# A fused decoder layer on one core: pair 1's softmax sums ahead of a split, a norm ahead of clearing, pair 2's output steps spread among the maxima

## The chip, the core and the metric

The kernel runs on one NeuronCore of one Trainium2 chip. Its engines are TensorE (PE, with its weight loads PEld), VectorE (DVE), ScalarE (ACT), GpSimd (POOL) and SyncE (SP, which here only issues DMAs). Each has an instruction stream of its own that runs in order; they meet at semaphores. The metric is device time in microseconds of one launch.

## The reference, cut to what matters

Inputs are 32 sequences of 64 tokens with 256 channels, and a context of the same shape. The layer is three sublayers, each followed by a residual sum and a layer norm:

```python
x = layernorm(x + self_attention(x))           # 16 heads of 16, causal
x = layernorm(x + cross_attention(x, ctx))     # 64 rows are channels, 256 columns positions: 8 heads of 8, rotary
x = layernorm(x + ffn(x))                      # bitlinear 256->1024, silu, gelu, norm, bitlinear 1024->256
```

The self attention of one pair of sequences is softmax(q k / 4) v, then the output matrix. The cross attention takes q from the normed result, k and v from the context, each projected and biased; q and k are rotated by position before their scores.

## The kernel before, in words

The work is cut into 16 pairs of sequences (`Pair`, `NPAIR`), 128 rows each. Phase A does both attentions, phase B the feed-forward part (from about 350 us on; the change doesn't touch it).

Phase A is a software pipeline. Each engine has a function `prologue()` and then `bodies(eng, body)`, which calls `body(i)` for i = -1, 0, ..., 15; the code is fully unrolled. Turn i has 16 steps s. In it pair i's exponentials are done (`exp_head` L683, `exp_tile` L886), the row maxima of the following tiles run 14 steps ahead (`AHEAD`; `max_head` L655, VectorE's `max_tile` L1080), pair i+2 gets its rotated queries, and pair a = i+3 its self attention. Turn -1 is special: from step 2 on it does the first 14 maxima of pair 0, the rotated queries of pair 1, the value projections for pair 0's cross attention (`xv_proj` L640), and the rest of pair 2's self attention. Pairs 0, 1 and the first half of 2 are done in `prologue()`.

The self attention of a pair goes through these steps, in this order of need:

- `qk_proj` (PE L560) into a bank, `qk_copy` (ACT L840), `k_mask` (L997, POOL, one of pair 0's on DVE), `scores` (PE L578 and L584) into g_b[0] and g_b[1]; before them the previous pair's first statistics instruction must have read g_b[1];
- `row_max` (DVE L1033), `minus_max` (DVE L1041) into `SP`, `self_exp` (ACT L858), `self_sum` (DVE L1050 and reciprocal L1052), `self_norm` (L1007, one instruction 128x1024; DVE for pair 0, POOL for the others);
- `transpose_p` (PE L597), `pt_copy` (ACT L865), `self_pv` (PE L610; it needs the value copies `v_copy`, ACT L848 and L851, and their crossing by DMA, `cross_values` L462), `ao_copy` (ACT L872), `out_proj` (PE L619);
- `norm1_stats` (DVE L1059, L1061, L1063), `rstd` (POOL L328 to L332), `norm1` (ACT L897).

For the cross attention `rotary_proj` (PE L632, L633) multiplies, `rotate` (DVE L1071) applies the tables, and `split_parts` (L1015 to L1025, five instructions, DVE for pair 0's queries, POOL otherwise) makes three bf16 parts. SyncE's `store_parts` (L437) writes them to HBM and `expand_rows` (L452) spreads them over the rows of `QA` and `KA`. Some rows of `KA` must hold ones before that: `ones_rows` (L1002, two memsets a call), for ring slots 0 and 2 on POOL and slot 1 on DVE. After the first eight maxima of a pair `max_transpose` (PE L669), `mt_copy` (ACT L880) and `mt_low` (DVE L1086) make rows that `max_rows` (L481) sends into `QA`; the exponentials of turn 0 need them.

The order on each engine is written out by hand, and an instruction waits for whatever stands before it on its engine. `idle_products(n)` (L791) issues n products of constants, 128x512 bf16, into the bank `u_b`, which nobody reads; they wait for nothing. VectorE's prologue before the change, around the moved lines:

```python
self_norm(dve, nc.vector, p0)
nc.vector.tensor_copy(identh[:], ident).then_inc(s_tab, 1)
ones_rows(nc.vector, 1)
norm1_stats(p0)
```

Of the kernel before, what the change touches and what calls it, by code (L numbers as in the profile page):

```python
# [80 lines left out]
def build_layer(nc, x, xT, ctx, wpT, woT, xW, xB, rows, w1T, w2T, attn_tables, rotary_tables, out):  # L81
    with ExitStack() as outer:
# [462 lines left out]
        def _(pe):  # L545
# [182 lines left out]

            pe.wait_ge(ld_wp, 16)

            def body(i):
                prev, nxt, j, a = i.plus(-1), i.plus(1), i.plus(2), i.plus(3)
                for s in range(16):
# [35 lines left out]
                    if s == 12 and real(a):  # L769
                        transpose_p(a)  # L770
                    if s == 13 and real(a):
                        self_pv(a)
                    if s == 13 and i.v == W_TOTAL:
                        weight_total(2)
                    if s == 15 and real(a):
                        out_proj(a)
                    for n, (turn, step) in enumerate(T_STEPS):
                        if i.v == turn and s == step:
                            pe.wait_ge(s_tab, 4)
                            numbers_transpose(pe, n, use(g_b[2], Event(s_tsb, 0), Pair(0, 0), n + 1)[:, :].bitcast(F16))  # L780
# [5 lines left out]

            def idle_products(n):


                for _ in range(n):  # L790
                    nc.tensor.matmul(u_b[:, :], identb[:], maskb[:].rearrange("p h s -> p (h s)"), start=True, stop=True)  # L791

            def prologue():
                p0, p1, p2 = (Pair(0, n) for n in range(3))
                qk_proj(p0, g_b[2])
                pe.wait_ge(ld_wv, 16)
                v_proj(p0, mx_b[0])
                rotary_proj("k", e_b[0], p0)
                pe.wait_ge(s_tab, 3)
                scores(p0)  # L800
                qk_proj(p1, g_b[2])
                pe.wait_ge(s_init, NINIT)
                idle_products(12)
                transpose_p(p0)
                idle_products(2)
                self_pv(p0)
                idle_products(2)
                out_proj(p0)
                idle_products(2)
                scores(p1)  # L810
                v_proj(p1, mx_b[0])
                idle_products(4)
                rotary_proj("q", mx_b[1], p0)
                rotary_proj("k", e_b[1], p1)
                qk_proj(p2, g_b[2])
                idle_products(12)
                transpose_p(p1)
                idle_products(2)
                self_pv(p1)
                idle_products(2)  # L820
                out_proj(p1)
                idle_products(2)
                scores(p2)
                v_proj(p2, e_b[0])
                rotary_proj("k", e_b[1], p2)
# [7 lines left out]
        def _(act):  # L833
# [93 lines left out]
            def prologue():  # L927
# [8 lines left out]
                norm1(p0)  # L936
                self_exp(p1, 1)
                self_exp(p1, 0)
                v_copy(p1, mx_b[0])
# [7 lines left out]
            def body(i):  # L947
                prev, nxt, j, a = i.plus(-1), i.plus(1), i.plus(2), i.plus(3)
                for s in range(16):
# [14 lines left out]
                    if s == 7 and fresh(a):  # L964
                        self_exp(a, 1)
                        self_exp(a, 0)
                    if s == 9 and real(nxt):
                        mt_copy(nxt, 0, 0)
                    if s == 12 and real(a):
# [3 lines left out]
                    if s == 13 and real(a):  # L973
# [55 lines left out]
        def _(dve):  # L1029
# [94 lines left out]
            def body(i):  # L1124
                prev, nxt, j, a = i.plus(-1), i.plus(1), i.plus(2), i.plus(3)
                for s in range(16):
# [15 lines left out]
                    if s == 9 and real(a):  # L1142
# [11 lines left out]
                    if s == 15 and real(a):  # L1154
# [14 lines left out]
            def prologue():  # L1169
# [10 lines left out]
                ones_rows(nc.vector, 1)  # L1180
# [5 lines left out]
                rotate("q", mx_b[1], p0)  # L1186
                split_parts(dve, nc.vector, "q", p0)
                self_sum(p1)
                rotate("k", e_b[1], p1)
                norm1_stats(p1)  # L1190
# [10 lines left out]
        def _(pool):  # L1201
# [15 lines left out]
            def prologue():  # L1217
# [5 lines left out]
                wait(pool, km[1], p1, 1)  # L1223
                ones_rows(nc.gpsimd, 2)
                pool.wait_ge(s_pad[2], 2)
                rstd(pool, ln1, p0, mv1, rs1)
                self_norm(pool, nc.gpsimd, p1)
# [4 lines left out]
            def body(i):  # L1232
# [6 lines left out]
                if i.v in (NPAIR - 3, NPAIR - 1):  # L1239
                    mean_power(pool, i.v // (NPAIR - 1))  # L1240
                if real(j):
                    split_parts(pool, nc.gpsimd, "q", j)
                if real(a):
# [420 lines left out]
```

## Time and profile before

| | |
|---|---|
| median of 3 runs | 528.34 us (527.87 to 529.71) |
| the profiled execution's own time | 528.22 us |
| its span | 525.7 us |
| TensorE busy | 427.8 us (81%) |
| VectorE busy | 439.2 us (84%) |
| ScalarE busy | 370.2 us (70%) |
| GpSimd busy | 294.2 us (56%) |

The span runs from the first to the last instruction; what lies around it, 2.5 us, is in the time but not in the trace. Busy times don't add up, as the engines work beside each other, and a share is a mean over stages: prologue and turn -1 (to about 62 us), the main loop (to about 350 us), the feed-forward part. A row of a timeline gives the start, the length, and in brackets how long the engine had been idle and what ended that. "PEclk" is the granted clock of TensorE as a share of full speed: 1.00 is 2.4 GHz, 0.50 is 1.2 GHz. Rows merge neighbouring instructions of the same kind, so "x4 2.47" is four in 2.47 us.

### The profile page before, as it was taken

The page shows a single profiled execution, that of the slowest core. Times are in us where ns is not written, and L with a number is a line of the kernel's source. Part 1 is how long each engine was busy: PE and PEld are TensorE (multiplying, and loading weights), DVE is VectorE, ACT ScalarE, POOL GpSimd, SP SyncE. Part 2 cuts the span into 40 slices and gives each one's busy share as a digit, 9 for nine tenths or more (in the row PEclk, how much of TensorE's full clock was granted, in tenths as well). Part 3 has the DMA queues.
Part 4 walks back from the last instruction along what each step waited for, and adds up shares of the span by engine and source line. Part 5 has one row for each costly group of instructions (what it writes and reads, how often), then busy time and mean ns, then how long its engine had stood idle before and what let it go on. Part 6 is the DMA issues. An engine that isn't in the chain of part 4 may idle for free. (4 is left out here: it accounts for less than half of the span.)

```text
span 525.7 us, 11922 instructions
## 1 busy us (share of the span) xinstructions
PE 427.8 (81%) x4130; PEld 231.0 (44%) x4138; DVE 439.2 (84%) x942; ACT 370.2 (70%) x690; POOL 294.2 (56%) x407
## 2 busy tenths in 40 slices
PE   6777899999999999999999999998996602555554
PEld 5453545555555555554545545443432101333332
DVE  2857697988979889799998998988877769999993
ACT  2232366778678786777877767677769878999983
POOL 6744566446474464745557455577232157667653
PEclk9998799999999999999999999999999855555557
DMA  6122313243252422424234232221000000000001
GB/s 222 50 78 65 108 42 112 67 137 113 68 153 66 138 75 65 148 56 139 76 95 144 57 109 63 68 83 52 3 2 0 1 0 1 21 21 20 32 31 40
DMA packets 52459, 37.05 MB, mean 70 GB/s; under 512 B 21552, under 2 KB 47792, under 8 KB 52400
## 3 DMA queue, kind: packets, MB, share of 16 engines
q1 hardware_dynamic: 52112, 36.06, 23.8%
q8 instruction: 33, 0.54, 0.4%
q10 hardware_dynamic: 288, 0.23, 0.2%
q14 instruction: 26, 0.21, 0.1%
HBM read 24.48 MB, written 10.49 MB: 67 GB/s over the span
## 5 line engine op out<-in xcount | busy, mean ns | idle before, releaser
L886 ACT ACTIVATE PB<-e_b 128x512 f32<-128x512 f32 x256 | 148.2, 592 | 59.1 <-PE e_b L683 58.0
L1080 DVE TENSOR_REDUCE MX<-mx_b 128x2 f32<-128x512 f32 x256 | 166.7, 678 | 25.3 <-PE mx_b L655 24.0
L655 PE MATMUL mx_b<-KA,QA 48*128 48x256 bf16 x512 | 98.1, 277 | 11.1 <-DVE MX L1080 10.7
L683 PE MATMUL e_b<-QA,KA 50*128 50x256 bf16 x512 | 97.3, 274 | 0.7 <-ACT PB L886 0.5
L700 PE MATMUL u_b<-PB,VA 128*32 128x256 f32 x1024 | 84.0, 391 | 2.0 <-ACT PB L886 1.7
L1007 POOL TENSOR_TENSOR SP<-SP,srec 128x1024 f32<-128x1024 f32 x15 | 28.5, 1901 | 77.7 <-DVE srec L1052 77.7
L655 PEld LDWEIGHTS mx_b<-KA,QA 48*128 48x128 bf16 x512 | 29.9, 94 | 86.0 <-issue 46.8
L1420 PE MATMUL r_b<-identh,Q 128*128 128x128 f16 x128 | 16.2, 306 | 39.4 <-ACT Q L1333 39.4
L1426 PE MATMUL z_b<-w2q,Q2T 128*128 128x256 bf16 x128 | 28.5, 400 | 19.3 <-ACT Q2T L1344 19.3
L997 POOL TENSOR_TENSOR KM<-QK,att_tab 128x512 f32<-128x512 f32 x31 | 32.0, 1053 | 21.2 <-ACT QK L840 21.2
L560 PE MATMUL g_b<-XT,wp 128*128 128x128 f32 x256 | 34.5, 291 | 4.5 <-DMA wp<-in_wpT 4.5
L1371 POOL TENSOR_TENSOR HHI<-HHI,row_tab 128x1024 f32<-128x1024 f32 x11 | 26.1, 2370 | 19.0 <-ACT HHI L1323 17.9
L700 PEld LDWEIGHTS u_b<-PB,VA 128*32 128x32 f32 x1024 | 22.5, 108 | 30.9 <-ACT PB L886 16.7
L560 PEld LDWEIGHTS g_b<-XT,wp 128*128 128x128 f32 x256 | 31.5, 200 | 7.7 <-DMA wp<-in_wpT 4.5
L1420 PEld LDWEIGHTS r_b<-identh,Q 128*128 128x128 f16 x128 | 12.2, 139 | 46.5 <-ACT Q L1333 46.4
L683 PEld LDWEIGHTS e_b<-QA,KA 50*128 50x128 bf16 x512 | 28.7, 94 | 7.7 <-ACT PB L886 3.6
L328 POOL TENSOR_TENSOR rs<-mv,epsc 128x1 f32<-128x1 f32 x32 | 6.1, 189 | 45.3 <-DVE mv L315 31.6
L865 ACT ACTIVATE PT<-g_b 128x512 f32<-128x512 f32 x32 | 17.5, 595 | 18.2 <-PE g_b L597 17.7
L1426 PEld LDWEIGHTS z_b<-w2q,Q2T 128*128 128x128 bf16 x128 | 15.9, 135 | 28.8 <-ACT Q2T L1344 23.4
L1033 DVE TENSOR_REDUCE smax<-g_b 128x8 f32<-128x512 f32 x32 | 20.6, 686 | 7.4 <-PE g_b L584 7.4
L1041 DVE TENSOR_TENSOR SP<-g_b,smax 128x512 f32<-128x512 f32 x32 | 21.5, 679 | 0.0
L1388 POOL TENSOR_TENSOR root<-base,halves 128x3 f32<-128x3 f32 x17 | 14.5, 856 | 12.4 <-DVE base L1549 12.2
(190 smaller groups left out, 1027.2 us busy)
## 6 DMA issues: line engine op xcount, KB each, us to landing
KA<-parts_k SPq DMA_DIRECT2D x64, 96.0 KB
QA<-parts_q SPq DMA_DIRECT2D x64, 96.0 KB
parts_q<-part_q SPq DMA_DIRECT2D x32, 128.0 KB, 1.9
parts_k<-part_k SPq DMA_DIRECT2D x16, 192.0 KB, 2.1
C<-in_ctx SPq DMA_DIRECT2D x16, 128.0 KB, 3.4
X<-in_x SPq DMA_DIRECT2D x16, 128.0 KB, 2.9
out_y<-O SPq DMA_DIRECT2D x16, 128.0 KB, 1.7
XT<-in_xT SPq DMA_DIRECT2D x15, 128.0 KB, 2.2
```

The costliest lines, as they stand in the source:

```text
L560: last = nc.tensor.matmul(ps[:, P * c:P * c + P], wp[:, k, P * c:P * c + P], XT[:, a.p, k, :], start=k == 0, stop=k == 1)
L655: m = nc.tensor.matmul(mx_b[n % 2][:, D * k:D * k + D], QA[low:low + K_MAX, 2 * i.ring + b, h, P * u:P * u + P], KA[low:low + K_MAX, 2 * i ...
L683: m = nc.tensor.matmul(e_b[n % 2][:, D * k:D * k + D], KA[low:low + K_EXP, 2 * i.ring + b, h, P * sc:P * sc + P], QA[low:low + K_EXP, 2 * ...
L700: last = nc.tensor.matmul(u_b[32 * j:32 * j + 32, D * b:D * b + D], VA[:, i.p, sc, b].rearrange("p h c -> p (h c)")[:, own:own + 32], PB[: ...
L886: nc.scalar.activation(PB[:, n % 4].rearrange("p e t -> p (e t)"), e_b[n % 2][:, :], ACT.Exp, scale=XC ** -0.5).then_inc(e_sb.sem, 1)
L997: ops.tensor_tensor(KM[:, c], QK[:, 2 + c, :].unsqueeze(1).broadcast_to([P, 4, P]), kmask.unsqueeze(2).broadcast_to([P, 4, P]), ALU.mult). ...
L1007: ops.tensor_tensor(SP[:], SP[:], srec[:].unsqueeze(2).broadcast_to([P, SH, SEQ]), ALU.mult).then_inc(s_norm.sem, 1)
L1041: nc.vector.tensor_tensor(SP[:].rearrange("p (c r k) s -> p c r k s", c=2, r=2)[:, :, r], g_b[r][:, :].rearrange("p (c k s) -> p c k s", c ...
L1080: nc.vector.tensor_reduce(MX[:, b, e, 2 * q:2 * q + 2, u], mx_b[n % 2][:, :].rearrange("p (e s) -> p e s", e=2), AXL.X, ALU.max).then_inc( ...
L1371: nc.gpsimd.tensor_tensor(row_h(i), row_h(i), gam, ALU.mult).then_inc(zg.sem, 1)
L1420: m = nc.tensor.transpose(r_b[j.p][:, P * k:P * k + P], low_half(Q2[:, j.p, P * k:P * k + P]), identh[:])
L1426: m = nc.tensor.matmul(z_b[j.p][:, 0:D], Q2T[:, j.p, k, :], w2q[:, k, :], start=k == 0, stop=k == 7)
```

## The change

On TensorE: in turn -1 `transpose_p`, `self_pv` and `out_proj` of pair 2 go from steps 12, 13 and 15 to 8, 9 and 11, and steps 2 to 11 of that turn each end with two idle products; in the prologue four idle products behind `v_proj(p1)` go, and twelve ahead of `transpose_p(p1)` become five. On ScalarE: `v_copy(p1)` goes ahead of `self_exp(p1)`, and pair 2's `pt_copy` and `ao_copy` go to step 8. On VectorE: `ones_rows` of slot 1 goes from ahead of pair 0's statistics to behind pair 1's key rotation; pair 1's sum and its normalisation, which was GpSimd's, come ahead of the queries' split; in turn -1 pair 2's sum goes from step 9 to step 4 and its statistics from step 15 to step 13. On GpSimd: pair 0's `rstd` goes ahead of `ones_rows` of slot 2, pair 1's `self_norm` is gone, and in turn -1 pair 2's `self_norm` goes ahead of the queries' split of pair 1. The number of instructions of the computation stays; idle products go from 40 to 49.

```diff
                         pe.wait_ge(f_sb, f_done(v - 1) - 1 + c)
                     m = first_half(pe, v, c, mx_b[c][:, :])
                 m.then_inc(f_ps.sem, 1)
+
+            def idle_products(n):
+
+
+                for _ in range(n):
+                    nc.tensor.matmul(u_b[:, :], identb[:], maskb[:].rearrange("p h s -> p (h s)"), start=True, stop=True)
 
             pe.wait_ge(ld_wp, 16)
 
...
                         max_transpose(nxt, 0, 0)
                     if s == 12 and real(i.plus(4)):
                         v_proj(i.plus(4), g_b[0])
-                    if s == 12 and real(a):
+                    if s == (12 if i.v >= 0 else 8) and real(a):
                         transpose_p(a)
-                    if s == 13 and real(a):
+                    if s == (13 if i.v >= 0 else 9) and real(a):
                         self_pv(a)
                     if s == 13 and i.v == W_TOTAL:
                         weight_total(2)
-                    if s == 15 and real(a):
+                    if s == (15 if i.v >= 0 else 11) and real(a):
                         out_proj(a)
+                    if i.v < 0 and 2 <= s < 12:
+                        idle_products(2)
                     for n, (turn, step) in enumerate(T_STEPS):
                         if i.v == turn and s == step:
                             pe.wait_ge(s_tab, 4)
...
                     for m in range(7):
                         if real(i) and pv_step(i.v, m) == 16 * i.v + s:
                             pv_quad(i, m)
-
-            def idle_products(n):
-
-
-                for _ in range(n):
-                    nc.tensor.matmul(u_b[:, :], identb[:], maskb[:].rearrange("p h s -> p (h s)"), start=True, stop=True)
 
             def prologue():
                 p0, p1, p2 = (Pair(0, n) for n in range(3))
...
                 idle_products(2)
                 scores(p1)
                 v_proj(p1, mx_b[0])
-                idle_products(4)
                 rotary_proj("q", mx_b[1], p0)
                 rotary_proj("k", e_b[1], p1)
                 qk_proj(p2, g_b[2])
-                idle_products(12)
+                idle_products(5)
                 transpose_p(p1)
                 idle_products(2)
                 self_pv(p1)
...
                 pt_copy(p0)
                 ao_copy(p0)
                 norm1(p0)
+                v_copy(p1, mx_b[0])
                 self_exp(p1, 1)
                 self_exp(p1, 0)
-                v_copy(p1, mx_b[0])
                 qk_copy(p2, g_b[2])
                 pt_copy(p1)
                 ao_copy(p1)
...
                     if s == 7 and fresh(a):
                         self_exp(a, 1)
                         self_exp(a, 0)
+                    if i.v < 0 and s == 8:
+                        pt_copy(a)
+                        ao_copy(a)
                     if s == 9 and real(nxt):
                         mt_copy(nxt, 0, 0)
-                    if s == 12 and real(a):
+                    if s == 12 and real(a) and i.v >= 0:
                         pt_copy(a)
                     if s == 13 and real(prev):
                         norm2(act, prev)
-                    if s == 13 and real(a):
+                    if s == 13 and real(a) and i.v >= 0:
                         ao_copy(a)
                     if s == 15 and real(i.plus(4)):
                         v_copy(i.plus(4), g_b[0])
...
                         minus_max(a, 1)
                     if s == 7 and fresh(a):
                         minus_max(a, 0)
-                    if s == 9 and real(a):
+                    if s == (9 if i.v >= 0 else 4) and real(a):
                         self_sum(a)
                     if s == 9 and real(a) and not fresh(a):
                         rotate("k", e_b[1], a)
...
                         norm2_stats(dve, prev, 1)
                     if s == 14 and real(prev):
                         norm2_max(dve, prev)
-                    if s == 15 and real(a):
+                    if s == (15 if i.v >= 0 else 13) and real(a):
                         norm1_stats(a)
                     if s == 14 and i.v == W_TOTAL:
                         weight_scale()
...
                 self_sum(p0)
                 self_norm(dve, nc.vector, p0)
                 nc.vector.tensor_copy(identh[:], ident).then_inc(s_tab, 1)
-                ones_rows(nc.vector, 1)
                 norm1_stats(p0)
                 row_max(p1, 1)
                 row_max(p1, 0)
                 minus_max(p1, 1)
                 minus_max(p1, 0)
                 rotate("q", mx_b[1], p0)
+                self_sum(p1)
+                self_norm(dve, nc.vector, p1)
                 split_parts(dve, nc.vector, "q", p0)
-                self_sum(p1)
                 rotate("k", e_b[1], p1)
+                ones_rows(nc.vector, 1)
                 norm1_stats(p1)
                 row_max(p2, 1)
                 row_max(p2, 0)
...
                 split_parts(pool, nc.gpsimd, "k", p0)
                 for c in range(2):
                     k_mask(pool, nc.gpsimd, p1, c, km)
-                wait(pool, km[1], p1, 1)
+                rstd(pool, ln1, p0, mv1, rs1)
+                wait(pool, ln1, p0, 6)
                 ones_rows(nc.gpsimd, 2)
                 pool.wait_ge(s_pad[2], 2)
-                rstd(pool, ln1, p0, mv1, rs1)
-                self_norm(pool, nc.gpsimd, p1)
                 for c in range(2):
                     k_mask(pool, nc.gpsimd, p2, c, km)
                 split_parts(pool, nc.gpsimd, "k", p1)
...
                         k_mask(pool, nc.gpsimd, a, c, km)
                 if i.v in (NPAIR - 3, NPAIR - 1):
                     mean_power(pool, i.v // (NPAIR - 1))
+                if i.v < 0:
+                    self_norm(pool, nc.gpsimd, a)
                 if real(j):
                     split_parts(pool, nc.gpsimd, "q", j)
-                if real(a):
+                if real(a) and i.v >= 0:
                     self_norm(pool, nc.gpsimd, a)
                 for v in {NPAIR - 3: range(0, 6), NPAIR - 2: range(8, 12)}.get(i.v, ()):
                     quantise(pool, v)
```

## Rows read from the trace of the kernel before

**Rows 1.** The page: TensorE's granted clock in 40 slices, in tenths.
```profile
PEclk9998799999999999999999999999999855555557
```

**Rows 2.** Windows: us from the start; busy us (instructions) of PE, PEld, DVE, ACT, POOL; PEclk; DMA share; GB/s.
```profile
40.00:42.00 2.00, 1.82 (x21) 0.74 (x19) 1.03 (x3) 0.00 (x0) 1.77 (x4) 1.00 0.01 5
44.50:48.00 3.50, 2.17 (x12) 1.02 (x12) 3.15 (x7) 1.43 (x3) 0.00 (x0) 1.00 0.17 47
44.70:61.60 16.90, 12.19 (x84) 7.01 (x86) 12.05 (x22) 4.16 (x11) 8.68 (x11) 0.70 0.34 90
48.00:58.20 10.20, 7.30 (x27) 4.42 (x28) 7.12 (x13) 0.98 (x3) 8.29 (x11) 0.50 0.27 68
84.00:340.00 256.00, 250.60 (x2710) 135.09 (x2708) 227.56 (x448) 189.26 (x417) 146.32 (x219) 1.00 0.34 97
403.00:406.40 3.40, 1.02 (x4) 0.32 (x4) 3.23 (x9) 3.37 (x7) 1.20 (x3) 1.00 0.00 0
406.40:409.80 3.40, 3.36 (x10) 1.25 (x10) 2.33 (x3) 3.13 (x4) 1.24 (x2) 0.50 0.00 0
```

**Rows 3.** Timeline of PE, prologue: start us, us, line, tiles, count, [idle before <-releaser].
```profile
21.73 1.10 PE L619 MATMUL g_b<-wout,AO 128*128 128x256 f32 x4
...
24.23 0.39 PE L578 MATMUL g_b<-maskb,identb 64*128 64x512 bf16 x2 [0.96 <-DVE Y L1059]
...
32.10 2.54 PE L791 MATMUL u_b<-maskb,identb 128*128 128x512 bf16 x11
35.94 1.09 PE L597 MATMUL g_b<-att_tab,SP 128*128 128x128 f32 x8 [1.31 <-POOL SP L1007]
...
39.10 1.10 PE L619 MATMUL g_b<-wout,AO 128*128 128x256 f32 x4
...
40.81 0.39 PE L578 MATMUL g_b<-maskb,identb 64*128 64x512 bf16 x2 [0.17 <-DVE Y L1059]
```

**Rows 4.** Timeline of DVE, prologue, same columns.
```profile
15.76 1.21 DVE L1050 TENSOR_REDUCE ssum<-SP 128x16 f32<-128x1024 f32 x1
...
17.29 1.22 DVE L1007 TENSOR_TENSOR SP<-SP,srec 128x1024 f32<-128x1024 f32 x1
...
21.86 1.76 DVE L1002 MEMSET KA<- 32x2048 bf16 x1 [0.48 <-issue]
23.66 0.42 DVE L1059 TENSOR_TENSOR Y<-g_b,X 128x256 f32<-128x256 f32 x1
...
26.92 1.28 DVE L1041 TENSOR_TENSOR SP<-g_b,smax 128x512 f32<-128x512 f32 x2
29.44 0.88 DVE L1071 SCALAR_TENSOR_TENSOR rot_q<-mx_b,xb_all,rot_tab 128x256 f32<-128x256 f32 x2 [1.25 <-PE mx_b L633]
...
32.41 1.21 DVE L1050 TENSOR_REDUCE ssum<-SP 128x16 f32<-128x1024 f32 x1
...
40.24 0.42 DVE L1059 TENSOR_TENSOR Y<-g_b,X 128x256 f32<-128x256 f32 x1 [5.63 <-PE g_b L619]
```

**Rows 5.** Timeline of ACT and of POOL around pair 0's norm.
```profile
27.55 0.60 ACT L897 ACTIVATE XALL<-Y,rs 128x256 f32<-128x256 f32 x1 [5.97 <-POOL rs L332]
...
22.60 3.65 POOL L1002 MEMSET KA<- 32x2048 bf16 x2
```

**Rows 6.** Timeline of PE from the first maxima to turn 0.
```profile
54.90 2.08 PE L569 MATMUL g_b<-wp,XT 128*128 128x256 f32 x4
...
61.58 0.28 PE L683 MATMUL e_b<-QA,KA 50*128 50x256 bf16 x1
...
64.10 0.28 PE L655 MATMUL mx_b<-KA,QA 48*128 48x256 bf16 x1
```

**Rows 7.** Timeline of DVE in turn -1.
```profile
44.70 2.47 DVE L1080 TENSOR_REDUCE MX<-mx_b 128x2 f32<-128x512 f32 x4
```

**Rows 8.** Timeline of SyncE's queue, end of turn -1.
```profile
54.65 1.23 SPq L481 DMA_DIRECT2D QA<-MR  x2
55.92 2.80 SPq L452 DMA_DIRECT2D QA<-parts_q  x4
```
## The prediction, made before the changed kernel ran

> **What bounds the kernel now.** I read four views in this order. First the strip of TensorE's granted clock: it is full except at slices 3 and 4 and in the tail [rows 1]. Then windows. From 84 to 340 us TensorE is busy 250.6 of 256 us [rows 2], so the main loop runs at the pace of its instruction list, and a loop that starts earlier ends earlier by as much. The prologue and turn -1, up to the first exponential-side product at 61.58 us, are different: there four engines hand small tiles to each other and each is idle in part, so I followed the hand-offs in the timelines [rows 3 to 8]. Two facts stand out. Pair 1's transposes on TensorE start at 35.94, released by GpSimd's normalisation, and everything of pair 2 comes behind them [rows 3]. And between 48.0 and 58.2 us the granted clock is 0.5, that is 1.2 GHz where it was 2.4, after a stretch (44.5 to 48.0) in which TensorE was busy 2.17 of 3.5 us with short products [rows 2]. There a product group 128x256 x4 takes 2.08 us [rows 6] against 1.10 at full clock [rows 3].
>
> **Step 1, pair 0's norm.** VectorE clears key rows (two instructions of 1.76 with 0.48 ahead of each, 4.5 us in all) before pair 0's statistics, which start at 23.66 [rows 4]. The product they read ends at 21.73 + 1.10 = 22.83 [rows 3]. With the clearing behind them they start at 22.9, 0.8 earlier, and so do pair 1's scores (24.23 to 23.45). GpSimd's own clearing (22.60 + 3.65 = 26.25) no longer precedes the reciprocal root; ScalarE's norm followed it at 27.55, 1.3 later [rows 5]. The root can now begin when the statistics end, about 24.0 (estimate: three VectorE instructions of about 0.4 or less from 22.9), so the norm starts at 25.3, 2.2 earlier. VectorE's rotation of the queries followed the norm's start by 1.9 (29.44) [rows 4] and could now start at 27.2. VectorE has its subtraction until 28.20 - 0.75 = 27.45 [rows 4], so the rotation starts at 27.45. The removed 4 idle products cost nothing and save nothing by themselves: TensorE then waited for the norm.
>
> **Step 2, pair 1's sums ahead of the split.** After the rotation (0.88) VectorE is free at 28.2; the exponentials end at about 28.1, as they follow the subtraction. The way from the sum to the normalisation is 17.29 - 15.76 = 1.53 us and VectorE's normalisation 1.22 [rows 4], where GpSimd's took until 35.9. So it ends at 28.2 + 1.53 + 1.22 = 30.95, and the transposes start at 31.0 instead of 35.94: 4.9 us earlier. Output product: 3.16 after the transposes (39.10 - 35.94), ends at 35.3 instead of 40.2 [rows 3]. The 12 idle products ahead of the transposes took 2.54 for the 11 that show [rows 3]; 5 take about 1.1 and fit before 31.0.
>
> **Step 3, where most of that is given back.** VectorE's queue is in order. Behind the normalisation now stand the queries' split (2.1 us: 29.44 + 0.88 to 32.41), the keys' rotation (0.88 at most) and the two clearing instructions (4.5) [rows 4], and only then pair 1's statistics. 30.95 + 2.1 + 0.8 + 4.5 = 38.3; I take 38.2. They stood at 40.24, waiting 5.63 us for TensorE; now TensorE's product lies ready from 35.3 and waits for VectorE. Of 4.9 us, 2.0 remain. TensorE's next work, pair 2's scores, needs those statistics to have read the bank (it started 0.57 after them), so 38.8 instead of 40.81. The queries' split of pair 0 ends 0.6 later than before (33.05 against 32.41), and with it their store and spread on SyncE. Before, the DMA engines had gone quiet by 40 (busy share 0.01 from 40 to 42) [rows 2], so these rows now land by about 40.7, under the 42 at which the first maximum wants them; this cover is 1.3 us, and without it the cost is what is missing of it. The rest of SyncE's order stands: pair 1's value crossing leaves earlier, its key store waits for SyncE rather than for GpSimd. The masks and the keys' split on GpSimd come 3 to 4 us earlier and are late nowhere. ScalarE's swap of the value copies and the exponentials costs nothing: the products they copy end before the subtraction does.
>
> **Step 4, turn -1.** The first maximum moves from 44.70 to 42.7 [rows 7]. From it to 61.58 were 16.9 us, with VectorE busy 12.05 and TensorE 12.19 [rows 2]. At full clock TensorE's part of it shrinks by half of the 7.30 it was busy in the low stretch, to 8.5, and 20 idle products at 0.21 add 4.3: 12.8 us. These lists give the lower bound 12.8 and the old distance the upper bound 16.9. Maxima are handed to and fro between both engines, two banks deep, so neither runs gapless. I walked the list in order with the durations of the rows: pair 2's sum after the third maximum (GpSimd normalises at 46, ahead of the queries' split), transposes at step 8, output product at step 11, and waits of 2 to 3 us on TensorE. That gives 15.5, so the exponentials start at 58.2, 3.4 earlier. 0.3 of this is lost at once: the first product of pair 1's maxima stands 2.5 behind now [rows 6] and 2.8 in my walk, because the last two maxima still wait for VectorE. **At full clock the gain is 3.1 us.** The idle products themselves cost 1 to 1.5 of it, by the same walk without them.
>
> **Step 5, the clock.** The change opens a hole on TensorE: from 35.7 (output product and two idle products) to 38.8 nothing runs, where the holes of before in the prologue were 0.17 to 1.5 us [rows 3]. The trace shows what came of thin stretches: after 2.17 busy of 3.5 us the clock fell for 10.2 us, and after 1.02 of 3.4 us (403.0 to 406.4) it fell for 3.4 us, in which TensorE was busy 3.36 [rows 2]. So I expect one fall near 37 to 40, ended soon because dense work follows (scores, values, rotation: 3.2 us at full clock). Price: nothing, if it doesn't fall, to 1.7 us (half of 3.4); I take 1.4, since the fall begins partly inside the hole and VectorE absorbs little. The page "TensorE: Matmul & The Clock Gate" of the Trainium skill (Part 1, and its section on oscillation) says that an idle TensorE is throttled and that activity releases it; by that rule the hole speaks against this change, and the sum is that with the fall, 1.7 instead of 3.1. The trace agrees so far as the two falls above go.
>
> **Sum.** -3.1 + 1.4 = -1.7, rounded to -1.8 for the 0.1 by which the walk of the kernel before began late. The profiled execution took 528.22 us (span 525.7 and 2.5 around it), 0.1 under the median of 528.34. 528.2 - 1.8 = **526.4 us**.
>
> **Rivals.**
> *No fall of the clock.* The hole lies so that the clock holds, as it held over holes of 1.5 us before. Against it: 3.1 us is longer than any hole in the full-clock prologue. Time: 528.2 - 3.1 = 525.1. Chance 0.25.
> *A second fall, or turn -1 no shorter.* From step 12 on there are no idle products, and TensorE waits for VectorE's statistics; the clock falls again near 57 to 60, when turn 0's dense list begins, for another 1 to 1.5 us. 526.4 + 1.2 = 527.6. Chance 0.14.
> *The transfer of pair 1's queries.* Its issue stands in SyncE's queue behind the maxima's rows (54.65, then 55.92) [rows 8]. In my walk those rows are ready 2.0 earlier, not 3.1, and the transfer's end isn't shown; if it landed just when used (64.10), the gain is capped at 2.0 even without a fall: 526.2. Chance 0.07.
> *Slower: the low clock stays through turn -1.* Place: from 38.8 on, with the 20 idle products in the queue ahead of the maxima, each then twice as long. A fall of 10.2 us as in the rows takes 5.1 us of work from TensorE, of which about 4.5 reach turn 0 or more if a second spell follows: 528.2 - 3.1 + 4.7 = 529.8. It decides from a low spell of about 7 us on; below that the gain outweighs it. For it: the only long spell in the loop's lead-in lasted that long. Against: that one had idle stretches in it, and here the list is dense. Chance 0.14.
> The forecast itself has 0.40, own range 525.8 to 527.2.
>
> **How the numbers follow.** A measurement of this kernel tells about 0.3%, 1.6 us: faster is below 526.8, slower above 529.9. Faster: 0.28 of the forecast's 0.40, plus 0.25 and 0.07, 0.60. Same: 0.12 + 0.14 + 0.02 = 0.28. Slower 0.12. The range goes from 524.5 (no fall, and 0.6 of the walk's uncertainty) to 529.3, leaving out the worse half of the slow case and the far end of the fast one.
>
> **What the profile would show.** Transposes of pair 1 at about 31 with VectorE as releaser; VectorE's clearing from 34 to 38 and pair 1's statistics directly behind it, no longer waiting for TensorE; TensorE idle 3 us ahead of pair 2's scores at 38.8; first maximum at 42.7; low clock somewhere in 37 to 42 and not in 48 to 58; first exponential product at 58 to 60. I am wrong if the transposes don't move by over 4 us, if the hole is under 2 us, or if turn -1 takes as long as before with the clock full. If the main loop gives back the earlier start, TensorE isn't its bound.

## The result and the profile after

The changed kernel takes 533.35 us (median of 8 executions, 530.02 to 535.29), the kernel before 528.31 (median of 8, 527.87 to 529.71): ratio 1.0079, 95% interval 1.0057 to 1.0100. It is 4 to 5 us slower where 1.8 less was forecast. The profiled execution took 531.77 us, 3.6 more than the profiled one before (528.22), and its span is 530.0, 4.3 more; the other 0.7 lies outside the spans. So the account below explains this execution, and the median is another 1.6 us longer. All differences of traces are of such single executions, and they are set against the first output product, which depends on nothing that changed: it starts at 21.30 here and at 21.73 before [rows 3], so 0.43 is added to a start of after when it is compared. One kernel below, the one without the idle products of turn -1, had two slow executions (535.55 and 537.02 us); they count in its median and not in its ratio.

VectorE's timeline of the changed kernel, prologue and first maximum (start us, us, line, tiles, count, idle before):

```profile
26.90 0.86 DVE L1075 SCALAR_TENSOR_TENSOR rot_q<-mx_b,xb_all,rot_tab 128x256 f32<-128x256 f32 x2
27.68 1.21 DVE L1054 TENSOR_REDUCE ssum<-SP 128x16 f32<-128x1024 f32 x1
...
29.22 1.23 DVE L1011 TENSOR_TENSOR SP<-SP,srec 128x1024 f32<-128x1024 f32 x1
30.36 1.26 DVE L1019 TENSOR_TENSOR full_q<-rot_q 128x256 f32<-128x256 f32 x1
31.55 1.25 DVE L1023 TENSOR_TENSOR part_q<-rot_q 128x256 bf16<-128x256 f32 x1
32.84 0.42 DVE L1025 TENSOR_TENSOR part_q<-full_q,part_q 128x256 bf16<-128x256 f32 x1
...
35.44 1.76 DVE L1006 MEMSET KA<- 32x2048 bf16 x1 [0.48 <-issue]
37.69 1.76 DVE L1006 MEMSET KA<- 32x2048 bf16 x1 [0.48 <-issue]
39.49 0.42 DVE L1063 TENSOR_TENSOR Y<-g_b,X 128x256 f32<-128x256 f32 x1
...
42.65 1.29 DVE L1037 TENSOR_REDUCE smax<-g_b 128x8 f32<-128x512 f32 x2 [2.06 <-PE g_b L584]
...
46.31 0.69 DVE L1084 TENSOR_REDUCE MX<-mx_b 128x2 f32<-128x512 f32 x1 [1.18 <-PE mx_b L655]
```

It answers to [rows 4]. Pair 1's sum and normalisation come before the split, as forecast; the memsets stand where they were expected, and pair 1's statistics (39.49) directly behind them, without a wait. But the first two instructions of the split take 1.26 and 1.25 us, against 0.42 for their fellows. GpSimd's timeline shows its two masks of pair 2 beside them:

```profile
30.12 2.40 POOL L1001 TENSOR_TENSOR KM<-QK,att_tab 128x512 f32<-128x512 f32 x2 [1.59 <-issue]
```

The first maximum is reduced at 46.31, where 42.7 was forecast.

TensorE's timeline of the same kernel:

```profile
30.50 1.09 PE L597 MATMUL g_b<-att_tab,SP 128*128 128x128 f32 x8
...
34.59 0.59 PE L733 MATMUL u_b<-maskb,identb 128*128 128x512 bf16 x2
40.06 0.61 PE L578 MATMUL g_b<-maskb,identb 64*128 64x512 bf16 x2 [4.87 <-DVE Y L1063]
40.60 1.98 PE L584 MATMUL g_b<-KM,QK 64*64 64x256 f32 x16
42.51 2.07 PE L569 MATMUL e_b<-wp,XT 128*128 128x256 f32 x4
...
45.88 0.39 PE L655 MATMUL mx_b<-KA,QA 48*128 48x256 bf16 x2
46.20 0.60 PE L733 MATMUL u_b<-maskb,identb 128*128 128x512 bf16 x2
46.74 0.39 PE L655 MATMUL mx_b<-KA,QA 48*128 48x256 bf16 x2
...
60.37 0.40 PE L655 MATMUL mx_b<-KA,QA 48*128 48x256 bf16 x4
61.55 0.39 PE L655 MATMUL mx_b<-KA,QA 48*128 48x256 bf16 x2 [0.78 <-DVE MX L1084]
63.13 0.39 PE L655 MATMUL mx_b<-KA,QA 48*128 48x256 bf16 x1 [1.20 <-DVE MX L1084]
63.14 0.39 PE L683 MATMUL e_b<-QA,KA 50*128 50x256 bf16 x1
...
64.27 3.78 PE L560 MATMUL g_b<-XT,wp 128*128 128x128 f32 x16
67.98 0.39 PE L655 MATMUL mx_b<-KA,QA 48*128 48x256 bf16 x1
```

It answers to [rows 3, 6]. The transposes start 5.0 us earlier; then TensorE does nothing for 4.9 us, and the scores behind that hole take 1.98 where 1.09 is usual, the value product 2.07 where it took 1.13 before. From 45.88 on it works without a gap through the maxima and idle products. It waits again only for the last maxima (0.78 and 1.20 us), and then pair 3's projections take 3.78 us where they took 2.05.

Windows of the changed kernel (columns as in [rows 2]):

```profile
35.20:40.00 4.80, 0.00 (x0) 0.00 (x0) 4.01 (x4) 0.00 (x0) 3.25 (x5) 0.86 0.36 106
38.80:45.50 6.70, 5.44 (x25) 3.38 (x26) 4.17 (x8) 0.83 (x4) 1.01 (x3) 0.50 0.35 106
46.00:60.00 14.00, 13.89 (x99) 6.50 (x98) 10.37 (x18) 3.24 (x8) 8.65 (x11) 1.00 0.21 54
62.70:69.30 6.60, 6.17 (x31) 4.26 (x32) 2.94 (x5) 2.30 (x5) 1.42 (x4) 0.50 0.44 133
84.00:340.00 256.00, 250.58 (x2738) 134.68 (x2727) 226.69 (x448) 189.90 (x418) 148.09 (x221) 1.00 0.35 99
```

There are two stretches at 1.2 GHz, each of about 6.8 us, in place of the one from 48 to 58. From 46 to 60 the clock is full and TensorE busy 13.9 of 14 us. The main loop is what it was: 250.58 us busy against 250.60.

Where the 4.3 us came from, in the same order:

| step | before | after (+0.43) | it adds |
|---|---|---|---|
| pair 1's statistics start | 40.24 | 39.92 | -0.3 |
| first maximum reduced | 44.70 | 46.74 | +2.4 |
| first exponential product | 61.58 | 63.57 | -0.1 |
| pair 1's first maximum product | 64.10 | 68.41 | +2.3 |

From there to the end it is 461.6 us before and 462.0 after. These 0.4 and the 0.43 by which this trace is ahead at the first output product cancel in the span.

### The profile page after: what moved, and what is told of

Its sections match the earlier page's. It is cut to its first block and busy times, and to the rows that moved or that the text cites. A ratio compares the mean times of both kernels' runs of the same rounds, so it can differ in the third digit from the quotient of the medians.

```text
span 530.0 us, 11947 instructions
## 1 busy us (share of the span) xinstructions
PE 433.0 (82%) x4147; PEld 231.5 (44%) x4147; DVE 442.6 (84%) x943; ACT 370.7 (70%) x690; POOL 293.4 (55%) x406
## 5 line engine op out<-in xcount | busy, mean ns | idle before, releaser
L1011 POOL TENSOR_TENSOR SP<-SP,srec 128x1024 f32<-128x1024 f32 x14 | 26.6, 1902 | 78.8 <-DVE srec L1056 78.8
L560 PE MATMUL g_b<-XT,wp 128*128 128x128 f32 x256 | 36.0, 299 | 4.7 <-DMA wp<-in_wpT 4.7
L560 PEld LDWEIGHTS g_b<-XT,wp 128*128 128x128 f32 x256 | 33.0, 208 | 8.0 <-DMA wp<-in_wpT 4.7
```

The source lines that it names most:

```text
L560: last = nc.tensor.matmul(ps[:, P * c:P * c + P], wp[:, k, P * c:P * c + P], XT[:, a.p, k, :], start=k == 0, stop=k == 1)
L1011: ops.tensor_tensor(SP[:], SP[:], srec[:].unsqueeze(2).broadcast_to([P, SH, SEQ]), ALU.mult).then_inc(s_norm.sem, 1)
```

## The experiments

All ratios are to executions of the kernel before that ran beside the changed one on the same chip. The kernels were measured in five groups, not all on one chip, in which the median of the kernel before was between 528.31 and 529.45 us, so two changed kernels are compared through their ratios. A ratio here is not the quotient of the two medians, and it differs from that by up to 0.002 (for the changed kernel the quotient is 1.0095); where the two disagree, a gain of that size is in doubt. Executions of one kernel scatter by several us, and each lists its granted clock. The time at the low clock is twice the span times what the mean clock lacks to 1. For the changed kernel it runs from 108.8 us in the execution of 530.02 to 122.7 in that of 535.29. So medians are given with their intervals, and small differences aren't leaned on.

| kernel | median us | ratio | interval |
|---|---|---|---|
| changed | 533.35 | 1.0079 | 1.0057 to 1.0100 |
| prologue's part alone | 529.20 | 1.0028 | 0.9996 to 1.0060 |
| turn -1's part alone | 530.66 | 1.0052 | 1.0019 to 1.0085 |
| no idle products in turn -1 | 529.70 | 1.0017 | 0.9984 to 1.0050 |
| slot 1's clearing on GpSimd | 528.90 | 1.0003 | 0.9972 to 1.0033 |
| both of these | 530.81 | 1.0021 | 0.9991 to 1.0050 |
| hole filled | 530.08 | 0.9994 | 0.9965 to 1.0024 |
| masks wait for the split | 529.49 | 0.9987 | 0.9951 to 1.0022 |
| idle products in steps 6 to 15 | 532.00 | 1.0033 | 1.0001 to 1.0065 |
| one idle product in steps 2 to 15 | 531.99 | 1.0040 | 1.0009 to 1.0070 |
| all mended, clearing on GpSimd | 526.36 | 0.9935 | 0.9907 to 0.9964 |
| all mended, masks wait | 525.60 | 0.9937 | 0.9907 to 0.9967 |
| kernel before, one idle product a step | 528.23 | 0.9966 | 0.9938 to 0.9995 |
| masks wait, old order in turn -1 | 526.00 | 0.9940 | 0.9914 to 0.9965 |
| clearing on GpSimd, old order | 528.43 | 0.9982 | 0.9954 to 1.0010 |

**The two halves of the change.** First only the changes of the four prologues, then only those of turn -1.

> The prologue's part of the change alone, turn -1 as before. Theory A (the hole behind VectorE's clearing lets TensorE's clock fall just when pair 2's dense products come, and the two slowed instructions of the split add 1.7 us): pair 2's scores start near 40 and run at 1.2 GHz, no gain, 529 to 532 us. Theory B (the idle products of turn -1 are the whole loss, the prologue by itself gains): 526 to 528 us.

> The prologue as before, only turn -1 as changed. Theory A (the loss is the prologue's): full clock through turn -1, and as that turn still takes 16.8 us, 527.5 to 529 us. Theory B (the loss is turn -1's: its idle products spread TensorE's list, and the thin steps 12 to 15 let the clock fall at the start of turn 0): low clock near 61 to 68, 530 to 533 us.

Turn -1's half alone costs 0.52%. The prologue's half shows 0.28%, with an interval that includes no change; the sum is about the whole, 0.79%. Neither theory was right alone. In the prologue's trace the clock is low from 38.6 to 45.5 and again from 52 to 59.5, and the first exponential product comes 1.6 us later than before, measured from the first output product. In turn -1's there is no fall until 62, yet the way from first maximum product to first exponential product is 17.26 us, against 17.50 before with 10.2 of it at 1.2 GHz.

**The clearing, and with it the hole.** The memsets of slot 1 move to GpSimd, behind its own of slot 2:

```diff
                 rotate("k", e_b[1], p1)
-                ones_rows(nc.vector, 1)
                 norm1_stats(p1)
...
                 ones_rows(nc.gpsimd, 2)
+                ones_rows(nc.gpsimd, 1)
                 pool.wait_ge(s_pad[2], 2)
+                pool.wait_ge(s_pad[1], 2)
```

> The change with VectorE's two clearing instructions of slot 1 done by GpSimd behind its own of slot 2. Theory A (the hole costs): pair 1's statistics start at about 35 instead of 39.5, no fall of the clock near 39, split without slowed instructions; 4.5 us from the queue and about 3 from the clock, 526 to 528.5 us. Theory B (the loss lies in turn -1 alone): the earlier start is kept but turn -1 and the fall behind it cost as much as before, 529 to 531 us.

TensorE's timeline of this kernel, around pair 2's scores:

```profile
33.81 1.10 PE L619 MATMUL g_b<-wout,AO 128*128 128x256 f32 x4
34.75 0.59 PE L733 MATMUL u_b<-maskb,identb 128*128 128x512 bf16 x2
35.52 0.39 PE L578 MATMUL g_b<-maskb,identb 64*128 64x512 bf16 x2 [0.18 <-DVE Y L1063]
35.84 1.09 PE L584 MATMUL g_b<-KM,QK 64*64 64x256 f32 x16
36.87 1.13 PE L569 MATMUL e_b<-wp,XT 128*128 128x256 f32 x4
...
40.88 0.39 PE L655 MATMUL mx_b<-KA,QA 48*128 48x256 bf16 x2 [2.02 <-DMA QA<-parts_q]
```

VectorE's and GpSimd's timelines, the split and what GpSimd does beside it:

```profile
30.52 0.42 DVE L1019 TENSOR_TENSOR full_q<-rot_q 128x256 f32<-128x256 f32 x1
25.03 7.35 POOL L1006 MEMSET KA<- 32x2048 bf16 x4
```

The scores start at 35.52 and at full clock: hole and fall are gone, and VectorE's split takes 0.42 an instruction, beside GpSimd's memsets. But 2.0 us come back at once, as the maxima now wait for pair 0's query rows. Here the cover under their transfer is used up. From the first maximum product to the first exponential product it is 17.26 us again, and the clock falls from 57 to 65. The best execution is 525.82 us, the median 528.90, between the ranges of the two theories.

**The hole alone.** Only TensorE's prologue is edited:

```diff
                 out_proj(p1)
-                idle_products(2)
+                idle_products(22)
```

> The change with 20 more idle products (4.3 us at full clock) in the hole between pair 1's output product and pair 2's scores, where TensorE waits for VectorE anyway. Theory A (the fall of the clock near 39 costs about 2.5 us): scores at the same 40.0 us but 1.4 long instead of 2.5, first maximum at about 43.5 instead of 45.9, time 2 to 3 us under the change. Rival (VectorE's lateness alone counts, the fall is absorbed): first maximum 0 to 1 us earlier, time as the change.

TensorE's timeline, from the added products to the first maximum:

```profile
34.94 4.91 PE L733 MATMUL u_b<-maskb,identb 128*128 128x512 bf16 x22
40.41 0.39 PE L578 MATMUL g_b<-maskb,identb 64*128 64x512 bf16 x2 [0.56 <-DVE Y L1063]
40.73 1.09 PE L584 MATMUL g_b<-KM,QK 64*64 64x256 f32 x16
41.75 1.13 PE L569 MATMUL e_b<-wp,XT 128*128 128x256 f32 x4
...
43.81 0.39 PE L655 MATMUL mx_b<-KA,QA 48*128 48x256 bf16 x2
```

The scores start as late as in the changed kernel (18.77 us after the first output product, 18.76 there), but the first maximum product 2.4 us earlier (22.17 against 24.58), and all of it is left at the first exponential product (39.44 against 41.84). That is the price of the fall as it came in the changed kernel's trace, 6.8 us long. The hole itself stays, and the ratio comes down from 1.0079 to 0.9994.

How long the fall lasts isn't fixed by the kernel. Two kernels further down have the same prologue as the changed one and the same hole of 4.87 us, and in their traces the clock was low for 3.4 us only, from 40.2 to 43.7 (no idle products in turn -1) and from 40.4 to 43.9 (idle products in steps 6 to 15). Their first maximum product comes 23.61 and 23.62 us after the first output product, 1.4 later than with the hole filled (22.17) and not 2.4.

**The contention.** One wait ahead of pair 2's masks on GpSimd:

```diff
                 pool.wait_ge(s_pad[2], 2)
+                wait(pool, split["q"], p0, 5)
                 for c in range(2):
                     k_mask(pool, nc.gpsimd, p2, c, km)
```

> The change with GpSimd's two masks of pair 2 made to wait until VectorE's split of pair 0's queries is done, so that the two don't run at the same time. If GpSimd's masks slowed the first two instructions of the split (1.26 and 1.25 us where 0.42 is usual), they take 0.42 again, pair 1's statistics start 1.7 us earlier, about 37.8, and the hole on TensorE shrinks by as much: time 1 to 2 us under the change. If the slow instructions have another cause, nothing moves.

VectorE's timeline of this kernel, split and statistics:

```profile
31.07 0.42 DVE L1019 TENSOR_TENSOR full_q<-rot_q 128x256 f32<-128x256 f32 x1
31.41 0.42 DVE L1023 TENSOR_TENSOR part_q<-rot_q 128x256 bf16<-128x256 f32 x1
31.86 0.42 DVE L1025 TENSOR_TENSOR part_q<-full_q,part_q 128x256 bf16<-128x256 f32 x1
...
38.52 0.42 DVE L1063 TENSOR_TENSOR Y<-g_b,X 128x256 f32<-128x256 f32 x1
```

GpSimd's timeline, the two masks:

```profile
33.35 2.04 POOL L1001 TENSOR_TENSOR KM<-QK,att_tab 128x512 f32<-128x512 f32 x2 [4.11 <-DVE part_q L1029]
```

With nothing running beside it the split takes 0.42 an instruction, and the statistics start at 38.52, 16.51 us after the first output product (22.01), against 18.19 in the changed kernel: 1.7 us earlier. On GpSimd the two masks took 2.40 in the changed kernel and take 2.04 here. The hole is 3.2 us long now, about what the prediction reckoned with (3.1), and in the profiled execution the clock didn't fall over it; it fell once under turn 0, from about 61.5 to 65.5. The ratio is 0.9987.

**The idle products of turn -1.** Four edits of the same two lines: they are left out; they are left out and the clearing is on GpSimd, as above; they stand in steps 6 to 15; or there is one in each of steps 2 to 15:

```diff
-                    if i.v < 0 and 2 <= s < 12:
-                        idle_products(2)
...
-                    if i.v < 0 and 2 <= s < 12:
+                    if i.v < 0 and 6 <= s:
                         idle_products(2)
...
-                    if i.v < 0 and 2 <= s < 12:
-                        idle_products(2)
+                    if i.v < 0 and 2 <= s:
+                        idle_products(1)
```

> The change without the 20 idle products of turn -1. Theory B (they cost more than they keep): the first exponential product comes 1.5 to 3 us earlier than in the changed kernel and the time is 530 to 532 us. Theory C (they keep the clock): the clock falls in the middle of turn -1 instead, for 7 to 10 us, and the time is that of the change or more, 533 to 536 us.

> The change with slot 1's clearing on GpSimd and without the 20 idle products of turn -1. If the hole in the prologue and the idle products are two separate losses (theory A and B together), both come back: at equal time spent at the low clock 2 to 3 us less than with the clearing on GpSimd alone, best executions 523 to 525 us. If TensorE's list wasn't the bound of turn -1, the same time as with the idle products, 526 at best.

> The change with its 20 idle products of turn -1 in steps 6 to 15 instead of 2 to 11: the same number, but the thin end of the turn is filled. If the second fall of the clock (62.6 to 69.4, under turn 0's dense list) comes from the thin end, it goes away and the time is 1.5 to 3 us under the change, with about 7 us less at the low clock. If not, the time is that of the change, and a fall appears in steps 2 to 5 at most.

> The change with one idle product in each of steps 2 to 15 of turn -1, 14 in all, in place of two in each of steps 2 to 11. The chain from first maximum to first exponential product was 17.3 us at full clock in every kernel with the 20. If TensorE's list is the bound there (0.54 us for two idle products), six fewer take 1.6 us off, 15.5 to 16 us at full clock, and time is 1.5 us under the change; if VectorE is, the 17.3 stay. The thin end being filled, the fall under turn 0 should be rarer.

Without any, the median is 529.70, and the times go from 527.49 up to 537.02. The trace is of this longest execution, with the clock low from about 50 to 61; of the other eleven only their total time at the low clock is known, 109 to 139 us against 109 to 123 in the changed kernel. Together with the clearing on GpSimd I had expected two gains to add up; they don't. All twelve executions have 125 us or more at the low clock, and in the trace it is low from 41 to 66. Its window of 46 to 60 us (columns as in [rows 2]), with TensorE busy 12.57 of 14 us and at 1.2 GHz throughout:

```profile
46.00:60.00 14.00, 12.57 (x70) 6.75 (x70) 7.31 (x15) 3.04 (x8) 7.47 (x11) 0.50 0.26 67
```

On this base the 20 products keep the clock: with them ten of twelve executions have less than 119 us at the low clock, without them none. What all 20 cost at full clock no trace shows, as every trace without them has the clock low in the turn. The late set does away with the fall under turn 0 in its trace (pair 3's projections take 2.05), as expected, but its time isn't the 530 to 531 that would follow: the clock falls later instead, between 368 and 379 us, and from pair 1's first maximum product to the end it is 466.0 us where it was 462.0 in the changed kernel. Of these 4.0 us, 2.3 are there when VectorE has done the last `HHI<-f_b` of the feed-forward part (357.2 us after that product, 354.9 in the changed kernel); the other 1.7 come in the tail (108.8 against 107.1), where the clock stays low to the end. Two windows of this kernel:

```profile
60.00:70.00 10.00, 9.68 (x88) 4.74 (x88) 7.58 (x15) 3.92 (x9) 4.93 (x8) 1.00 0.41 120
360.00:380.00 20.00, 17.95 (x156) 7.65 (x151) 12.56 (x24) 12.62 (x26) 6.67 (x14) 0.74 0.07 21
```

With fourteen single products, first maximum product to first exponential product is 16.2 us (45.84 to 62.02), 1.1 less for six products less, so they had cost time. By itself that doesn't show in the median (531.99); the hole and the contention are still in it, and in its trace the fall at the hole (6.8 us), one under turn 0 (3.4) and one near 370 (6.8).

**Everything mended, and the kernel before with single products.** To the clearing on GpSimd, and to the waiting masks, are added:

```diff
                 rotary_proj("k", e_b[1], p2)
+                idle_products(8)
...
                 out_proj(p1)
-                idle_products(2)
+                idle_products(14)
```

The first goes with the clearing on GpSimd (under the wait for the query rows), the second with the waiting masks (in what is left of the hole).

> All that was found put together: slot 1's clearing on GpSimd (no hole, no slowed split), 8 idle products under the 2.0 us wait for pair 0's query rows, one idle product in each of steps 2 to 15. First maximum at 40.9, first exponential product at 56 to 57, no fall of the clock before 60: median 524 to 526 us, 2 to 4 under the kernel before. If falls of the clock elsewhere (near 370, or under turn 0) take it back, 527 to 529 and a wide spread.

> The change with GpSimd's masks waiting for the split, the rest of the hole filled with 12 more idle products, and one idle product in each of steps 2 to 15: first maximum at 42.4, first exponential product near 58, 525 to 527 us. If the hole's length rather than its emptiness cost the time, no better than with the masks' wait alone (526.7 at best, 529.5 in the median).

> The kernel before with one idle product in each of steps 2 to 15 of turn -1 and nothing else. If the low clock of 48 to 58 us cost the kernel before anything, it goes away and the first exponential product comes 1 to 2 us earlier, 526.5 to 527.5 us. If idle products only take what the full clock gives, as the 20 did in the changed turn, the time is that of the kernel before.

In all three the single products are the last edit above (for the kernel before, its only one). TensorE's timeline of the version with the waiting masks:

```profile
35.20 3.19 PE L733 MATMUL u_b<-maskb,identb 128*128 128x512 bf16 x14
38.98 0.39 PE L578 MATMUL g_b<-maskb,identb 64*128 64x512 bf16 x2 [0.60 <-DVE Y L1063]
...
42.25 0.39 PE L655 MATMUL mx_b<-KA,QA 48*128 48x256 bf16 x2
42.57 0.39 PE L733 MATMUL u_b<-maskb,identb 128*128 128x512 bf16 x1
42.89 0.39 PE L655 MATMUL mx_b<-KA,QA 48*128 48x256 bf16 x2
...
58.51 0.28 PE L655 MATMUL mx_b<-KA,QA 48*128 48x256 bf16 x1 [0.76 <-DVE MX L1084]
...
59.43 2.05 PE L560 MATMUL g_b<-XT,wp 128*128 128x128 f32 x16
61.42 0.28 PE L655 MATMUL mx_b<-KA,QA 48*128 48x256 bf16 x1
```

Both mended versions beat the kernel before by 0.6%, and by their ratios the changed kernel by 1.4%. The first missed part of what was expected of it: its first maximum product comes 19.8 us after the first output product where the clearing on GpSimd alone had 19.4, and in its trace, of its longest execution, the clock falls at 58.5 and again near 370. In the trace of the second one TensorE's clock doesn't fall before 403 us, and pair 1's first maximum product comes at 61.42, 39.51 us after the first output product; before it was 42.37, in the changed kernel 46.68. The kernel before gains 0.34% by single products alone, with an interval that ends just short of no change, and its median only 0.13% (528.23 against 528.93): its first exponential product comes 1.2 us earlier, in the stretch where its clock had been low.

**The order inside turn -1.** The last two kernels take the mended versions and put the output steps back to 12, 13 and 15, the sum to 9, the statistics to 15, and with them ScalarE's copies and GpSimd's order in that turn.

> As the version with waiting masks, filled hole and one idle product a step, but with the old order inside turn -1 (output steps at 12, 13 and 15, sum at 9, statistics at 15). If the new order ends turn -1 thinly and so makes TensorE's last maxima wait and the clock fall under turn 0, the distance from the first exponential product to pair 1's first maxima is 2.5 us instead of 2.9, no fall near 60, and the time is 0.5 to 1.5 us under the new order's. If the new order brings what it looks like (pair 2's steps among the maxima), the old one is 1 us or more slower.

> The same test with slot 1's clearing on GpSimd and 8 idle products under the wait for the query rows: old order inside turn -1. New order thin at its end: 0.5 to 1.5 us under the version with the new order, and rarely a fall near 58. New order useful: 1 us or more over it.

The distance from the first exponential product to pair 1's first maximum product is 2.5 us with the old order (59.03 to 61.55, 59.84 to 62.37), 2.9 with the new one at full clock (58.52 to 61.42). There is no fall near 60, but one at 52 to 56 in both. On the first base the times are equal (526.0 and 525.6), on the second the old order is 2 us slower. The expected distances came, the expected gain didn't: the new order's thin end is real, but the old one has its thin place earlier. That the order as such gains or loses is not shown.

## Why the prediction was wrong

The step that failed first is step 3: it took the split's time from a stretch in which GpSimd was idle. Three further terms were too small. The terms are compared at pair 1's first maximum product: forecast -1.7 (-3.1 and 1.4 for the clock), measured +4.3, so 6.0 are missing.

- **Step 1 and step 2 held.** Norm, sums, transposes: 30.50 + 0.43 = 30.9, 31.0 forecast.
- **Step 3, the split, +1.7.** I took the split's 2.1 us from a stretch in which GpSimd stood still, and moved the masks beside it (they come "3 to 4 us earlier and are late nowhere") without asking what two engines do to each other. Put at nothing without a reason, it was 1.7 us, as the wait in front of the masks shows. The Trainium skill has the rule, on the page "SBUF — State Buffer" in the section "Who interferes with whom": a VectorE instruction with two SBUF inputs contends with a GpSimd instruction that reads SBUF, and not with one that only writes it. The traces agree on both points: the split's first two instructions took 1.26 and 1.25 us beside the masks, 0.42 with GpSimd idle, and 0.42 beside its memsets in the kernel with the clearing there.
- **Step 5, the clock, +1.0.** The place was right: a fall that began in the hole, 4.9 us long because of the split. It lasted 6.8 us and not 3.4, and cost 2.4 instead of 1.4, as the filled hole shows. The price for 3.4 us was right: the two traces in which the fall was that short lose 1.4. Which length comes is a matter of the execution, so the 1.0 is luck as much as a wrong term. But for the hole of 3.1 us that was reckoned with, the fall itself isn't shown: over the 3.2 us of the waiting masks the clock held in the one trace there is, as the first rival had it.
- **Step 4, turn -1, +1.3.** 16.8 us from the first reduction on instead of 15.5. The walk gave the idle products 0.21 each, from a run of eleven of their own kind, so 0.43 a pair. Between two maxima a pair takes 0.54 (46.20 to 46.74 in TensorE's rows), 1.1 more for ten pairs. TensorE was busy 13.89 of the 14 us from 46 to 60, so its list and not VectorE's set the turn up to there; the last two waits, 0.78 and 1.20, are for VectorE. Six products fewer take 1.1 off. That the dearer pairs are the whole 1.3 is an estimate.
- **The second rival came true, +2.0.** The fall under turn 0 (chance 0.14) added 2.3 us where my walk had 0.3: thin steps 12 to 15, and then a dense list at 1.2 GHz. The rival had just this, a second fall on top of the first, but priced it at 1.2. Even with it the time would have been 527.6, as the other terms were still short.

1.7 + 1.0 + 1.3 + 2.0 = 6.0. The slower rival, one long low spell through the turn, isn't what happened: with the 20 products the clock was full there. The range had a place for two falls at these low prices (527.6), but none for the split's 1.7 or for the idle products' dearer pairs.

## What to carry to other kernels

Filling TensorE to hold its clock is cheapest where it would have waited: idle products in a hole cost nothing and gave 2.4 us, as many in its busy list took what the full clock gave, and fourteen single ones there still gave the kernel before 1.2 us. When work moves forward, look at who now stands behind the long in-order neighbour, and at what runs beside the moved instructions on the other engine: a duration read in quiet isn't the duration in company. Falls of the clock at separate places add up: with the first one gone the second stayed, and the way from the first exponential product to pair 1's first maximum product was 4.84 us long either way. Price each thin stretch by itself, and judge such changes by many executions.

## What the runs showed of the hardware that was not expected

- A fall of the clock doesn't stay where it was, nor keep its length. Seven of the fourteen traces of the experiments have one near 370 us, 300 us after the edits, where the traces of the two main kernels have none. Two short ones left nothing at the end: with 3.4 us at the low clock there, from pair 1's first maximum product to the end it is 461.8 us in the kernel with turn -1's part alone and 461.5 in the kernel before with single products, against 461.6. With 10.2 us, in the kernel with the late idle products, 2.3 us were left.
- The scatter between executions goes with the time at the low clock: for the kernel before, measured beside the two halves, 112.4 to 112.8 us of it go with 527.2 to 529.7 us, two executions with 115.9 took 528.5 and 529.5, and 118 to 130 go with 529.3 to 533.4.
- Idle products are dearer in between than in a row: 0.54 for two between maxima, 0.43 for two in a run (22 in 4.91 us, the last of them 0.38).
- VectorE's two-input instruction of 0.42 us took 1.25 beside GpSimd's mask, while GpSimd's two lost 0.36 in all.
